# Moving GpSimd's word load behind a gather, and building the second pass's edge one-hots from TensorE's squares

## The chip, the cores and the metric

The kernel runs on one core of a Trainium2 chip. The metric is device time in microseconds. The kernel before takes 11216.39 us (median of 3 runs, 11213.91 to 11227.2); the execution that was profiled took 11191.52 us, and its span in the trace is 11189.8 us.

## The reference

Four graph layers over 6250 nodes of 128 features and 200,000 edges, sorted by destination. Each layer is `x = x + layer(relu(layernorm(x)))`. Their edge work, cut to what matters:

```python
# layer 0: typed attention, 4 heads         # layer 1: GAT, 4 heads
a   = (kw[e] * q[dst]).sum(-1) * pri        a = leaky_relu(a_src[src] + a_dst[dst], 0.2)
att = exp(a - max_dst(a)) / sum_dst         att = exp(a - max_dst(a)) / sum_dst
agg = segment_sum(msg * att, dst)           out = segment_sum(xh[src] * att, dst)
# layer 2: graph convolution                # layer 3: clipped attention, 8 heads
agg = segment_sum(h[src] * deg, dst)        s = exp(clip(K[src].Q[dst] / 4, -5, 5)); sum V[src] * s
```

Between them stand dense products over the 49 blocks of 128 nodes.

## The kernel before, in words

**Four edge passes.** Each layer has one pass over all edges: `softmax_pass` for layers 0 and 1 (called with `dot` true and false), `conv_pass` for layer 2, `clipped_pass` for layer 3. Edges come in 392 groups of 512, each group in four tiles of 128. A group whose edges end in more than one block of 128 destination nodes is visited once for each block, so there are 440 visits. Every engine has a program of its own, unrolled over 12 or 16 visits in a loop, and they are coupled by semaphores alone.

**GpSimd's program (`fetch`, L449).** For each of the 392 groups it issues four indirect gathers (L464), one for each tile of 128 edges, from a table in DRAM (`kv_typed`, `gat_rows`, `conv_rows`, `kv_rows`) into one of 14 slots of a ring in SBUF (`edges_rows`). Behind each gather stands a `pause` (L467), an addition on a tile of 128x56. That makes 1568 gathers and as many pauses in a pass. A slot may be filled again when the visits that read it are over. How many visits that is depends on the data, and stands in a table in SBUF (`seat_rows`). At the first group of each half ring (7 groups) GpSimd's sequencer loads 7 of these words into registers (`TENSOR_LOAD`, L377), and then waits, ahead of each group, for the semaphore `used` to reach the group's word. The loop runs over 14 groups, so half of the loads stand at the head of a turn of the loop.

**A visit of the softmax passes.** TensorE multiplies five feature rows per edge (`feat_r`) with a constant (`col_feat`): the result in `ps_near` is the squared distance of each edge's destination from each of the 128 nodes (`squares`, L587). ScalarE turns it into a one-hot, `relu(1 - x)`, with nodes in the partitions (`pick_tb`, L705, and for `dot` also `pick_t`). The other orientation, with edges in the partitions (`pick_b`), is made by VectorE: it compares a row 0..127 with each edge's local number (`make_pick`, L754; the tile lies in the space of `x` in the first pass and of `q` in the second). ScalarE widens `pick_b` to f32 (`widen_pick`, L665) for the sums that TensorE makes eight visits later (`sum_rows`, L615); VectorE adds them to the running sums (L812) after fading these (L806). In the second pass VectorE also makes one-hots that count the sources (`count`, L897), and weighs the gathered rows (`weigh`, L797). VectorE works through a visit in the order that `body` at L899 writes out.

## Time and profile before

| | busy us | share of the span |
|---|---|---|
| GpSimd (POOL) | 8748.9 | 78% |
| TensorE (PE) | 6661.3 | 60% |
| VectorE (DVE) | 5435.4 | 49% |
| ScalarE (ACT) | 2291.9 | 20% |
| span / time of the profiled execution | 11189.8 / 11191.52 | |

Busy counts the engine itself. Loads of registers, branches, semaphores and the issuing of DMAs are the sequencer's and not counted, so they show only as idle time of the engine ahead of its next instruction. For GpSimd, a gather (`DMA_INDIRECT`) is counted as busy. The passes are found by the table that the gathers read: the first gather of a pass starts, and the last one ends, at 537.3 and 3009.2 us (layer 0), 3187.1 and 5834.2 (layer 1), 6024.5 and 8469.1 (layer 2), 8631.8 and 11075.1 (layer 3).

### The profile page before, as it was taken

To read this page: it belongs to the slowest core of one execution; us is meant where nothing else is said; L and a number is where in the kernel's file an instruction comes from. 1 tells how busy PE (TensorE), PEld (TensorE's weight loads), DVE (VectorE), ACT (ScalarE), POOL (GpSimd) and SP (SyncE) were. 2 spreads that over 40 slices of the span, in tenths; PEclk is the share of its full clock that TensorE was granted. 3 is DMA by queue.
4 is the path that set the end of the run, shared out by engine and by line. 5 is a ranking of instruction groups with operands and counts; after the bars stand their busy time and mean duration, and the time that the engine had idled before them with its cause. 6 is when DMAs were issued, how large, how long until landed. Compare 5 with 4: busy or idle time off the path is not lost. (4 is left out here: it accounts for less than half of the span.)

```text
span 11189.8 us, 165217 instructions
## 1 busy us (share of the span) xinstructions
PE 6661.3 (60%) x36530; PEld 5305.4 (47%) x36531; DVE 5435.4 (49%) x14242; ACT 2291.9 (20%) x6368; POOL 8748.9 (78%) x12683
## 2 busy tenths in 40 slices
PE   5867777777755555555554333333336767776767
PEld 3656556556534444444443333333333555555554
DVE  4266666666666565566554111111113555555555
ACT  1333333333342222222223000000002111111111
POOL 0188888888758888888876888888883888888885
PEclk9966666767765555555556555555555666666667
DMA  3332222222211111111121111111111332222222
GB/s 114 141 87 84 85 85 85 85 86 85 78 43 42 42 42 41 42 42 43 42 49 34 43 43 42 43 43 43 43 43 52 87 86 85 85 85 85 85 85 65
DMA packets 379796, 731.69 MB, mean 65 GB/s; under 512 B 169786, under 2 KB 219249, under 8 KB 373270
## 3 DMA queue, kind: packets, MB, share of 16 engines
q0 software_dynamic: 251264, 621.88, 21.3%
q1 hardware_dynamic: 100906, 98.01, 2.7%
q10 hardware_dynamic: 27500, 10.39, 0.4%
q8 instruction: 46, 0.75, 0.0%
q14 instruction: 80, 0.66, 0.0%
HBM read 652.95 MB, written 76.88 MB: 65 GB/s over the span
## 5 line engine op out<-in xcount | busy, mean ns | idle before, releaser
L467 POOL TENSOR_TENSOR edges_pause<-edges_pause 128x56 f32<-128x56 f32 x6272 | 2094.7, 334 | 120.0
L464 POOL DMA_INDIRECT edges_rows<-gat_rows,edges_idx_r x1568 | 1743.7, 1112 | 326.2 <-issue 301.8
L464 POOL DMA_INDIRECT edges_rows<-conv_rows,edges_idx_r x1568 | 1628.7, 1039 | 331.7 <-issue 320.6
L464 POOL DMA_INDIRECT edges_rows<-kv_typed,edges_idx_r x1568 | 1596.3, 1018 | 332.6 <-issue 313.5
L1005 PE MATMUL edges_ps_sum<-edges_rows,edges_pick 128*128 x3520 | 889.1, 435 | 1580.5 <-POOLq L470 1551.9
L464 POOL DMA_INDIRECT edges_rows<-kv_rows,edges_idx_r x1568 | 1520.5, 970 | 332.1 <-issue 322.7
L615 PE MATMUL edges_ps_sum<-edges_wv,edges_pick 128*128 128x132 f32 x7040 | 1676.2, 410 | 30.1 <-issue 17.6
L615 PEld LDWEIGHTS edges_ps_sum<-edges_wv,edges_pick 128*128 128x128 f32 x7040 | 1433.4, 298 | 368.4 <-issue 340.2
L1005 PEld LDWEIGHTS edges_ps_sum<-edges_rows,edges_pick 128*128 128x128 f32 x3520 | 773.6, 325 | 1695.8 <-issue 1695.7
L1103 PE MATMUL edges_ps_q<-q,edges_pick_t 128*128 x3520 | 751.8, 381 | 726.2 <-DVE edges_prod L1167 644.1
L1025 DVE TENSOR_TENSOR sums<-sums,edges_ps_sum 128x129 f32 x440 | 127.7, 290 | 2038.8 <-PE edges_ps_sum L1005 1684.3
L1103 PEld LDWEIGHTS edges_ps_q<-q,edges_pick_t 128*128 128x128 f32 x3520 | 650.6, 276 | 828.6 <-issue 828.1
L1093 PE MATMUL edges_ps_sum<-edges_wv,edges_pick 128*128 128x136 f32 x3520 | 810.1, 399 | 7.9 <-DVE sums L1189 7.8
L597 PE MATMUL edges_ps_q<-q,edges_pick_t 128*128 x3520 | 760.9, 379 | 58.9 <-issue 40.0
L1093 PEld LDWEIGHTS edges_ps_sum<-edges_wv,edges_pick 128*128 128x128 f32 x3520 | 693.4, 284 | 164.7 <-issue 161.6
L597 PEld LDWEIGHTS edges_ps_q<-q,edges_pick_t 128*128 128x128 f32 x3520 | 658.7, 277 | 96.1 <-issue 89.9
L797 DVE TENSOR_TENSOR edges_wv<-edges_rows,edges_wv 128x512 f32<-128x512 f32 x880 | 618.3, 703 | 1.5 <-ACT edges_wv L657 1.4
L1167 DVE TENSOR_TENSOR edges_prod<-edges_rows,edges_ps_q 128x512 f32<-128x512 f32 x440 | 301.6, 685 | 620.6 <-issue 339.7
L1157 DVE TENSOR_TENSOR edges_pick<-edges_ps_iota,edges_local 128x512 f32<-128x512 f32 x440 | 304.5, 692 | 546.5 <-issue 516.5
L754 DVE TENSOR_TENSOR x<-iota_bf,edges_local 128x512 bf16<-128x512 bf16 x440 | 314.4, 714 | 481.3 <-issue 398.0
L1134 ACT ACTIVATE edges_wv<-edges_gap 128x32 f32<-128x32 f32 x440 | 113.1, 257 | 2123.4 <-DVE edges_gap L1196 1756.4
L657 ACT ACTIVATE edges_wv<-edges_gap 128x16 f32<-128x16 f32 x880 | 200.8, 228 | 1543.8 <-issue 1149.9
(343 smaller groups left out, 10567.2 us busy)
## 6 DMA issues: line engine op xcount, KB each, us to landing
kv_typed<-l0pre_out SPq DMA_DIRECT2D x49, 1024.0 KB
edges_rows<-kv_typed,edges_idx_r POOLq DMA_INDIRECT x1568
edges_rows<-gat_rows,edges_idx_r POOLq DMA_INDIRECT x1568
edges_rows<-conv_rows,edges_idx_r POOLq DMA_INDIRECT x1568
edges_rows<-kv_rows,edges_idx_r POOLq DMA_INDIRECT x1568
edges_feat_r<-visit_features ACTq DMA_DIRECT2D x660, 10.0 KB
kv_rows<-l3pre_kv SPq DMA_DIRECT2D x7, 896.0 KB
edges_flag_r<-visit_flags ACTq DMA_DIRECT2D x220, 16.0 KB
```

The costliest lines, as they stand in the source:

```text
L464: pool.indirect_dma_start(rows[:, k, g * width:(g + 1) * width], None, table, bass.IndirectOffsetOnAxis(ap=idx_r[:, k, g:g + 1], axis=0)). ...
L467: nc.gpsimd.tensor_tensor(pause, pause, pause, ALU.add).then_inc(paused, 1)
L597: mm = nc.tensor.matmul(ps_q[s % 2][:, g * D:(g + 1) * D], pick_t[:, s % 2, g * P:(g + 1) * P], q[:, bass.ds(b * D, D)], start=True, stop= ...
L615: mm = nc.tensor.matmul(ps_sum[s % 2][:, 0:aw], pick[:, s % 2, g * P:(g + 1) * P], wv[:, s % 3, g, :], start=g == 0, stop=g == G - 1)
L657: nc.scalar.activation(wv4[:, s % 3, :, :, hd], gap[:, s // SPAN, j * GH:(j + 1) * GH].rearrange("p (g h) -> p g h", g=G), ACT.Exp).then_i ...
L754: nc.vector.tensor_tensor(pick_b[:, s, :].rearrange("p (g n) -> p g n", g=G), c["iota_bf"].unsqueeze(1).broadcast_to([P, G, P]), bcast(loc ...
L797: nc.vector.tensor_tensor(wv4[:, s % 3, :, :, 0:hd], vals, bcast(wv4[:, s % 3, :, :, hd], [P, G, heads, hd]), ALU.mult).then_inc(wv_done, 1)
L1005: mm = nc.tensor.matmul(ps_sum[k % banks][:, 0:aw], pick[:, k % deep, g * P:(g + 1) * P], now[:, g, :], start=g == 0, stop=g == G - 1)
L1093: mm = nc.tensor.matmul(ps_sum[s % 2][:, 0:aw], pick[:, s % 6, g * P:(g + 1) * P], wv[:, s % 3, g, :], start=g == 0, stop=g == G - 1)
L1103: mm = nc.tensor.matmul(ps_q[s % 2][:, g * D:(g + 1) * D], pick_t[:, s % 2, g * P:(g + 1) * P], q[:, bass.ds(b * D, D)], start=True, stop= ...
L1157: nc.vector.tensor_tensor(pick[:, s % 6, :].rearrange("p (g n) -> p g n", g=G), ps_iota[:, 0:P].unsqueeze(1).broadcast_to([P, G, P]), bcas ...
L1167: nc.vector.tensor_tensor(prod[:].rearrange("p (g d) -> p g d", g=G), of_slot(rows, slot, width)[:, :, 0:D], ps_q[s % 2][:].rearrange("p ( ...
```

## The change

Two things. First, in `fetch` the load of the words moves behind the first gather of the half ring, ahead of that gather's pause. It then holds the words of the next seven groups, and not of the half ring's own. The first group of a half ring waits for nothing any more: its word is waited for one group earlier (`k % HALF == HALF - 1`), in place of that group's own, smaller word. This holds for all four passes.

Second, in the second pass (`dot` false) VectorE no longer makes `pick_b`. TensorE makes a second set of squares, transposed, from the same feature rows: four products of 128 columns into a new bank `ps_pick`, and ScalarE turns it into `pick_b` with a second activation. There is now one bank `ps_near` in that pass instead of two, squares are made two visits ahead instead of three, and `local` is not loaded.

```diff
@@ fetch
         if k % HALF == 0:
             pool.wait_ge(idx_in[k // HALF], it * 16 + 16)
-            if known(j, SLOTS):
-                visits[:] = words(pool, res, 3, j - SLOTS, HALF)
-        if known(j, SLOTS):
-            pool.wait_ge(used, at_least_one(pool, visits[k % HALF], NV))
+        elif k % HALF == HALF - 1 and known(j + 1, SLOTS):
+            pool.wait_ge(used, at_least_one(pool, visits[HALF - 1], NV))
+        elif known(j, SLOTS):
+            pool.wait_ge(used, at_least_one(pool, visits[k % HALF - 1], NV))
         pool.sem_inc(slot_free, 1)
         for g in range(G):
             pool.indirect_dma_start(...)
+            if g == 0 and k % HALF == 0 and known(j + HALF, SLOTS):
+                early = max(SLOTS - 1 - j, 0) if isinstance(j, int) else 0
+                visits[:] = [None] * early + list(words(pool, res, 3, j + 1 - SLOTS + early, HALF - early))
             pool.wait_ge(paused, j * G + (g + 1))
             nc.gpsimd.tensor_tensor(pause, pause, pause, ALU.add).then_inc(paused, 1)
@@ softmax_pass, tensor: squares
-                    if known(u, 2):
-                        pe.wait_ge(pick_tb_done, u - 1)
-                    nc.tensor.matmul(ps_near[s % 2][:], c["col_feat"], feat_r[:, s // 2 % 3, s % 2], start=True,
-                                     stop=True).then_inc(squares_done, 1)
+                    near = feat_r[:, s // 2 % 3, s % 2]
+                    if known(u, near_banks):
+                        pe.wait_ge(pick_tb_done, u + 1 - near_banks)
+                        if not dot:
+                            pe.wait_ge(pick_b_done, u)
+                    mm = nc.tensor.matmul(ps_near[s % near_banks][:], c["col_feat"], near, start=True, stop=True)
+                    if not dot:
+                        for g in range(G):
+                            mm = nc.tensor.matmul(ps_pick[:, g * P:(g + 1) * P], near[:, g * P:(g + 1) * P], c["col_feat"], start=True, stop=True)
+                    mm.then_inc(squares_done, 1)
-                    to_square, to_spread, last, ninth = (wide_at(i, k, it, d) for d in (3, 1, -1, -9))
+                    to_square, to_spread, last, ninth = (wide_at(i, k, it, d) for d in (3 if dot else 2, 1, -1, -9))
@@ softmax_pass, scalar: one_hots
                     if s % SPAN == 0 and known(u, WIDE):
                         act.wait_ge(ref_done, t * 3 + s // SPAN - 2)
+                        if not dot:
+                            act.wait_ge(top_part, t * 3 + s // SPAN - 2)
-                    nc.scalar.activation(pick_tb[:, s, :], ps_near[s % 2][:], ACT.Relu, bias=1.0, scale=-1.0).then_inc(pick_tb_done, 1)
+                    nc.scalar.activation(pick_tb[:, s, :], ps_near[s % near_banks][:], ACT.Relu, bias=1.0, scale=-1.0).then_inc(pick_tb_done, 1)
+                    if not dot:
+                        nc.scalar.activation(pick_b[:, s, :], ps_pick[:], ACT.Relu, bias=1.0, scale=-1.0).then_inc(pick_b_done, 1)
@@ softmax_pass, vector
-                    if now:
+                    if dot and now:
                         make_pick(now)
-                    if dot and now:
                         multiply_q(now, slot, due)
-                dve.wait_ge(local_in, 16)
+                if dot:
+                    dve.wait_ge(local_in, 16)
```

GpSimd's program at the head of a turn of the second pass's loop, before. `ISA` rows are arithmetic on registers, `L377` belongs to the words, `L386` checks a word and waits with it:

```order
L467 TENSOR_TENSOR edges_pause<-edges_pause 128x56
L367 UNCONDITIONAL_BRANCH
L367 BRANCH_PREFETCH_HINT
L367 ISA
L377 ISA
L377 TENSOR_LOAD seat_rows
L386 ISA x2
L464 DMA edges_rows<-gat_rows,edges_idx_r 128x132
L466 ISA
L467 TENSOR_TENSOR edges_pause<-edges_pause 128x56
```

The same place now:

```order
L470 TENSOR_TENSOR edges_pause<-edges_pause 128x56
L367 UNCONDITIONAL_BRANCH
L367 BRANCH_PREFETCH_HINT
L367 ISA
L464 DMA edges_rows<-gat_rows,edges_idx_r 128x132
L377 ISA
L377 TENSOR_LOAD seat_rows
L469 ISA
L470 TENSOR_TENSOR edges_pause<-edges_pause 128x56
L464 DMA edges_rows<-gat_rows,edges_idx_r 128x132
```

The load stood between a pause and a gather; it stands between a gather and its pause.

VectorE's program for one visit of the second pass, before (L754 is `make_pick`, L806 the fading, L897 the source counts, L797 the weighing):

```order
L377 TENSOR_LOAD seat_rows
L754 TENSOR_TENSOR q<-iota_bf,edges1_local 128x512
L806 ISA
L806 TENSOR_TENSOR sums<-sums,edges1_fade 128x132
L897 TENSOR_TENSOR edges1_lo_hot<-iota_bf,edges1_src_lo 128x512
L897 TENSOR_TENSOR edges1_hi_hot<-iota_bf,edges1_src_hi 128x196
L797 ISA
L797 TENSOR_TENSOR edges1_wv<-edges1_rows,edges1_wv 128x16x32
L821 TENSOR_TENSOR edges1_ends<-edges1_ps_turn,last_rows 128x64
L812 TENSOR_TENSOR sums<-sums,edges1_ps_sum1 128x132
```

The same visit now (all lines behind the changed ones are numbered 16 higher):

```order
L377 TENSOR_LOAD seat_rows
L822 ISA
L822 TENSOR_TENSOR sums<-sums,edges1_fade 128x132
L913 TENSOR_TENSOR edges1_lo_hot<-iota_bf,edges1_src_lo 128x512
L913 TENSOR_TENSOR edges1_hi_hot<-iota_bf,edges1_src_hi 128x196
L813 ISA
L813 TENSOR_TENSOR edges1_wv<-edges1_rows,edges1_wv 128x16x32
L837 TENSOR_TENSOR edges1_ends<-edges1_ps_turn,last_rows 128x64
L828 TENSOR_TENSOR sums<-sums,edges1_ps_sum1 128x132
```

Only `make_pick` is gone there. TensorE's program for a visit of the second pass, now, in which the row L599 is new:

```order
L616 MATMUL edges1_ps_q<-a_dst,q 128x12 x4
L596 MATMUL edges1_ps_near0<-edges1_feat_r,col_feat 128x512
L599 MATMUL edges1_ps_pick<-col_feat,edges1_feat_r 128x128 x4
L627 MATMUL edges1_ps_sum1<-edges1_wv,edges1_pick 128x132 x4
L635 MATMUL edges1_ps_hist<-edges1_hi_hot,edges1_lo_hot 128x49 x4
```

The four new products stand between the squares and the sums.

## Rows read from the trace of the kernel before

**Rows 1.** The passes: length; PE, PEld, DVE, ACT, POOL busy; clock, DMA share, GB/s.
```profile
537.30:3009.20 2471.90, 1782.65 (x11088) 1445.76 (x11086) 1602.56 (x4231) 835.89 (x2175) 2113.51 (x3135) 0.68 0.30 85
3187.10:5834.20 2647.10, 1488.05 (x11111) 1190.08 (x11111) 1588.83 (x4905) 720.18 (x2173) 2297.22 (x3135) 0.50 0.19 42
6024.50:8469.10 2444.60, 886.97 (x3512) 771.78 (x3512) 402.53 (x878) 0.00 (x0) 2087.65 (x3135) 0.52 0.19 43
8631.80:11075.10 2443.30, 1713.17 (x7447) 1374.21 (x7447) 1274.99 (x2628) 323.41 (x878) 2084.24 (x3135) 0.65 0.30 85
```

**Rows 2.** GpSimd by line, each pass: busy us, mean ns, idle ahead and its releasers.
```profile
L464 POOL DMA_INDIRECT edges_rows<-kv_typed,edges_idx_r x1568 | 1596.3, 1018 | 332.6 <-issue 313.5 <-DVE edges_wv L797 15.0 <-DMA edges_idx_r<-typed_sources 4.1
L467 POOL TENSOR_TENSOR edges_pause<-edges_pause 128x56 f32<-128x56 f32 x1567 | 517.3, 330 | 29.9
...
L464 POOL DMA_INDIRECT edges_rows<-gat_rows,edges_idx_r x1568 | 1743.7, 1112 | 326.2 <-issue 301.8 <-DVE edges_wv L797 17.1 <-DMA edges_idx_r<-sources 6.8
L467 POOL TENSOR_TENSOR edges_pause<-edges_pause 128x56 f32<-128x56 f32 x1567 | 553.6, 353 | 30.4
...
L464 POOL DMA_INDIRECT edges_rows<-conv_rows,edges_idx_r x1568 | 1628.7, 1039 | 331.7 <-issue 320.6 <-PE edges_ps_sum L1005 6.8 <-DMA edges_idx_r<-sources 4.4
L467 POOL TENSOR_TENSOR edges_pause<-edges_pause 128x56 f32<-128x56 f32 x1567 | 459.0, 293 | 29.6
...
L464 POOL DMA_INDIRECT edges_rows<-kv_rows,edges_idx_r x1568 | 1520.5, 970 | 332.1 <-issue 322.7 <-DVE edges_wv L1174 6.3 <-DMA edges_idx_r<-sources 3.1
L467 POOL TENSOR_TENSOR edges_pause<-edges_pause 128x56 f32<-128x56 f32 x1567 | 563.8, 360 | 30.0
```

**Rows 3.** Waits of GpSimd's gathers, whole span: us, times, longest us.
```profile
POOL edges_rows L464 <- DVE edges_wv L797: 32.1, 20, 1.8
```

**Rows 4.** Line 377, word loads (ns min/median/max, start): all; the one before 6588.
```profile
L377 POOLq TENSOR_LOAD <-seat_rows x216: 1591/1601/1808, 618.8 to 11031.7; - x108
...
L377 POOLq TENSOR_LOAD <-seat_rows x1: 1594/1594/1594, 6587.0 to 6587.0; - x1
```

**Rows 5.** Timeline (start, us, idle ahead) of GpSimd, load inside a turn.
```profile
6585.64 0.96 POOL L464 DMA_INDIRECT edges_rows<-conv_rows,edges_idx_r  x1 [0.16 <-issue]
...
6587.06 0.96 POOL L464 DMA_INDIRECT edges_rows<-conv_rows,edges_idx_r  x1 [0.16 <-issue]
6588.04 0.29 POOL L467 TENSOR_TENSOR edges_pause<-edges_pause 128x56 f32<-128x56 f32 x1
6589.65 0.96 POOL L464 DMA_INDIRECT edges_rows<-conv_rows,edges_idx_r  x1 [1.33 <-issue]
```

**Rows 6.** The same around a load at the head of a turn.
```profile
6981.36 0.96 POOL L464 DMA_INDIRECT edges_rows<-conv_rows,edges_idx_r  x1 [0.16 <-issue]
...
6984.42 1.42 POOL L464 DMA_INDIRECT edges_rows<-conv_rows,edges_idx_r  x1 [1.79 <-PE edges_ps_sum L1005]
```

**Rows 7.** Timeline of the second pass, GpSimd and VectorE in a long gather.
```profile
4034.69 3.32 POOL L464 DMA_INDIRECT edges_rows<-gat_rows,edges_idx_r  x1 [1.74 <-DVE edges_wv L797]
4034.82 0.67 DVE L754 TENSOR_TENSOR q<-iota_bf,edges_local 128x512 bf16<-128x512 bf16 x1
4035.42 0.28 DVE L806 TENSOR_TENSOR sums<-sums,edges_fade 128x132 f32 x1
...
4037.66 0.23 DVE L830 TENSOR_TENSOR edges_split<-edges_ends,edges_split 128x64 bf16<-128x64 f32 x1
```

**Rows 8.** Groups by line in the second pass.
```profile
L754 DVE TENSOR_TENSOR q<-iota_bf,edges_local 128x512 bf16<-128x512 bf16 x440 | 309.2, 703 | 191.8 <-issue 148.4 <-ACT edges_pick L665 43.4
...
L587 PE MATMUL edges_ps_near<-edges_feat_r,col_feat 5*128 5x512 bf16 x440 | 264.8, 602 | 0.0
L705 ACT ACTIVATE q<-edges_ps_near 128x512 bf16<-128x512 f32 x440 | 258.4, 588 | 92.0 <-issue 71.3 <-PE edges_ps_near L587 20.5
```

**Rows 9.** Timeline of TensorE in the second pass, its sums of consecutive pairs.
```profile
4032.29 2.13 PE L615 MATMUL edges_ps_sum<-edges_wv,edges_pick 128*128 128x132 f32 x8
...
4035.80 2.13 PE L615 MATMUL edges_ps_sum<-edges_wv,edges_pick 128*128 128x132 f32 x8
```

11 lines of the change are left out of this document (7 added, 4 removed).

## The prediction

> **What bounds the kernel now.** I read the busy shares first: GpSimd has 78% of the span. Then the passes one by one. In each of the four GpSimd is busy for 2084 to 2297 us of 2443 to 2647, 85 to 87%, and every other engine for at most 72% [rows 1]. Next, GpSimd's own groups: a pass is 1568 gathers and their pauses, the means are 970 to 1112 ns and 293 to 360 ns, and the idle time ahead of the gathers is "issue", not a wait for somebody's work [rows 2]. Check: 1743.7 + 553.6 + 326.2 + 30.4 = 2653.9, the second pass with the 6.8 us ahead of its first gather. The waits that are put down to VectorE's `edges_wv` are 20 in the span and none is over 1.8 us [rows 3]; these are 1.8 us because a word load stands there, as the next views show. So GpSimd runs back to back, the passes last as long as its stream, and a microsecond taken out of it shortens the kernel. The chain that ended last tells nothing here, as it covers only the last dense stage.
>
> GpSimd's beat is read in the timeline: from gather to gather 6587.06 - 6585.64 = 1.42 us, with 0.16 us idle ahead of a gather [rows 5]. Ahead of the first gather of a half ring it is idle for 1.33 us inside a turn of the loop [rows 5] and 1.79 at its head [rows 6]. The cause is the word load: 216 of them, all about 1.60 us [rows 4]. The sequencer issues it when the gather before starts (6587.0 against 6587.06 [rows 4, 5]), so 1.26 us of it lie beside that gather and its pause; it ends at 6588.6, and the next gather starts 1.04 us behind that.
>
> **Term A, the load, in all four passes.** Before, 54 loads a pass: 27 at (1.33 - 0.16) and 27 at (1.79 - 0.16) are 31.6 + 44.0 = 75.6 us. The other way round, from [rows 2] for the third pass: 331.7 - 4.4 (its first wait) - 1568 x 0.16 = 76.4. Both agree; in the second pass it is 326.2 - 6.8 - 250.9 = 68.5, as its long gathers cover some of it.
> After: the load stands behind a gather and ahead of its pause, in program order. The gather is issued, the load starts with it as before (0.04 us ahead) and ends at 1.56 us on the gather's clock; one register instruction and the pause's dispatch, 0.1 us estimated, put the pause at 1.66 to 1.70 in place of 0.98 (6588.04 - 6587.06). It delays the next gather by 0.70 us. The first gather of the half ring itself now follows at 0.16: the loop's branch and the wait for the indices, 0.46 us (1.79 - 1.33), lie beside a gather and a pause of 1.26. There is one more load (group 7, one word): 55 x 0.70 = 38.5 us a pass. Saved: 75.6 - 38.5 = 37 us in three passes and 68.5 - 38.5 = 30 in the second, together 141 us. So the move does not take away the load; it drops the tail of 1.04 us behind it for 0.1 us and the branch in its shadow, but gives up the pause as cover.
> Bounds: nothing is paid for the tail or the pause waits for nothing of the load: 4 x 75 = 295 us. If the load's tail of 1.04 us goes along with it, the delay is 1.56 + 1.04 - 1.42 + 0.28 + 0.16 = 1.62 us, 55 x 1.62 = 89 a pass, and A is a loss of 4 x 14 = 54 us. I take 141: no gather's address and no check of a word stands between load and pause now, as the order shows.
> The wait for a later word, one group early, costs nothing: GpSimd does not wait for a word today [rows 3]. What hides it is a ring of 14 slots; if that cover were gone, each half ring would wait for up to one group, 4 x 1.42 = 5.7 us.
>
> **Term B, VectorE off GpSimd's back, in the second pass.** VectorE's `make_pick` is 440 x 703 ns = 309 us [rows 8]. VectorE is busy for 60% of this pass [rows 1], so that alone buys nothing. But GpSimd's own instructions are stretched: the gathers' mean is 1112 ns against 1039 in the third pass, whose table has rows of nearly the same width (132 and 129 words), and the pauses' 353 against 293 [rows 2]: 1568 x 0.073 + 1567 x 0.060 = 114 + 94 = 208 us. A gather of 3.32 us shows how: it starts at 4034.69, VectorE starts `make_pick` at 4034.82 and then works without a break until 4037.89, and the gather ends at 4038.01, 0.12 us behind [rows 7]; the usual is 0.96 [rows 5]. In that chain `make_pick` is 0.67 of 3.07 us, 22%. If the stretching shrinks with VectorE's time, B = 0.22 x 208 = 46 us. If the second pass becomes like the first, it is more: the first against the fourth (two tables of rows of 256 words) is 1568 x 0.048 - 1567 x 0.030 = 28 us, so nearly all of 208 would go, the upper end. The lower end: the third pass, too, has a `make_pick` a visit and the stretching is measured against it, so that `make_pick` alone may be worth nothing. I take 60, above the proportional 46, because `make_pick` is what the break in VectorE's work is missing: it opens the chain, and without it VectorE waits there.
> The Trainium skill ("SBUF — State Buffer", Who interferes with whom) says that a VectorE instruction with two inputs in SBUF holds GpSimd up only where that reads SBUF, and infers that the writing of descriptors is not held by such a one. The trace disagrees with the second half, with its gather of 3.32 us [rows 7]. By the rule only the pauses would gain, 0.22 x 94 = 21 us in place of 60.
>
> **Term C, the new work.** TensorE: four products of 128 columns, as many columns as the one of 602 ns [rows 8], 0.6 us a visit and 264 us in all; ScalarE: one more activation of 588 ns [rows 8], 259 us. With them TensorE is busy for 1750 of 2600 us and ScalarE for 980. When rows have come, TensorE goes through its visits at 35.80 - 32.29 = 3.5 us each [rows 9]; this becomes 4.1, while GpSimd delivers a visit each 2647 / 440 = 6.0 us. So the work is hidden by 1.9 us a visit, and costs 0.6 x 10 visits, at most 6 us, in the tail behind the last gather. I take 3. What the cover is worth: each 0.1 us by which a visit passes 6.0 costs 44 us.
>
> **Sum.** 141 + 60 - 3 = 198 us off the profiled execution's 11191.5: 10993. The median is 25 us above that execution, and I carry that along: 11216 - 198 = 11018 us. A difference under 0.2%, 22 us, counts as no change.
>
> **Rivals.**
> 1. *The load carries its tail along.* A is -54, B 60: 11216 - 3 = 11213, no change. For it: today every gather behind a load comes 1.04 us late. Against: that tail holds the check of a word and the gather's address, and neither stands behind the load now. Chance 0.07.
> 2. *The port is freed for good.* VectorE's chains break up, B is 150: 11216 - 141 - 150 + 3 = 10928. For it: the first pass has no such stretching. Against: the source counts and the weighing stay, 2.4 of the chain's 3.07 us. Chance 0.14.
> 3. *`make_pick`'s place is taken by what follows it.* B is 0 to 20: 11216 - 141 - 10 + 3 = 11068. For it: GpSimd meets another VectorE instruction at once. Against: the chain is shorter in any case. Chance 0.17. The Trainium skill's rule above ("SBUF — State Buffer", Who interferes with whom) would leave the gathers as they are and so points to this case.
> 4. *Slower: the single bank makes the second pass TensorE's.* TensorE may write `ps_near` only when ScalarE has read both banks of the visit before. If squares (1.2 us), two activations (1.2) and the sums with their rest (2.9) came one behind the other with waits between, a visit would take over 6.0 us and GpSimd would wait for slots. At 6.8 us the pass lasts 440 x 6.8 = 2992, 345 more than 2647: 11216 + 345 - 111 (A of the other passes) = 11450. It decides from 6.02 us. Against: ScalarE reads the squares in the visit in which TensorE makes them and the next come one visit later, so the sums lie between. Chance 0.03.
>
> **How the numbers follow.** The forecast, 10975 to 11055, has 0.56; rival 1 0.07, 2 0.14, 3 0.17, 4 0.03; the remaining 0.03 is a load wholly hidden, 11216 - 295 - 60 + 3 = 10864. The range 10925 to 11115 takes in rivals 2 and 3 at their times and leaves out 1, 4, the hidden load and a part of 2. Faster: 0.56 + 0.14 + 0.17 + 0.03 and a quarter of rival 1, 0.92; same 0.05; slower 0.03.
>
> **What would show it.** In the second pass, `ps_pick` products and a second activation; GpSimd's idle time ahead of its gathers at 250 to 262 us a pass, and that ahead of the pauses at 30 + 38 = 68 (before 30); in the timeline a pause 0.7 us behind its gather's end each half ring. Gathers and pauses of the other three passes unchanged in length; in the second, gathers under 1.09 us and pauses under 0.34. The passes at 2435, 2557, 2408 and 2406 us. It is wrong if the idle time only moves from gathers to pauses (rival 1), if the gathers of the second pass stay above 1.10 us (rival 3), or if GpSimd waits for `used` there (rival 4).

## The result and the profile after

The changed kernel takes 10847.47 us (median of 4 runs, 10836.52 to 10850.32), the kernel before 11218.1 beside it. The ratio is 0.9667, 95% interval 0.965 to 0.9683: faster by 371 us, where 198 were forecast. The time lies below the forecast range. The profiled execution took 10849.15 us, its span is 10847.4. The trace of the kernel before is of an execution of 11191.52 us that is not among the four runs behind those 11218.1, so differences of a few us between the two traces can be those of two chips.

The table of passes of the changed kernel answers to [rows 1], with the same columns:

```profile
537.20:2944.70 2407.50, 1748.33 (x11088) 1424.08 (x11086) 1605.28 (x4231) 838.30 (x2175) 2110.58 (x3135) 0.70 0.30 87
3121.00:5558.00 2437.00, 1644.74 (x12746) 1325.34 (x12746) 1372.00 (x4419) 931.36 (x2591) 2102.94 (x3135) 0.50 0.20 46
5766.60:8166.80 2400.20, 889.66 (x3512) 774.37 (x3512) 402.92 (x878) 0.00 (x0) 2111.68 (x3136) 0.52 0.20 44
8330.90:10730.90 2400.00, 1720.68 (x7446) 1378.65 (x7447) 1274.36 (x2628) 323.31 (x878) 2096.64 (x3135) 0.65 0.30 87
```

The passes are shorter by 64, 210, 44 and 43 us; what lies between and behind them is longer by 20. So 152 us come from the three passes that only the load's move touches, and 210 from the second. Forecast were 37, 90, 37 and 37: of the 161 us between 201 and 362, 120 lie in the second pass and 27 in the first.

GpSimd by line in each pass answers to [rows 2] (busy us, mean ns, idle ahead and its releasers):

```profile
L464 POOL DMA_INDIRECT edges_rows<-kv_typed,edges_idx_r x1568 | 1604.6, 1023 | 264.5 <-issue 260.2 <-DMA edges_idx_r<-typed_sources 4.2
L470 POOL TENSOR_TENSOR edges_pause<-edges_pause 128x56 f32<-128x56 f32 x1567 | 506.0, 323 | 36.6 <-issue 6.7
...
L464 POOL DMA_INDIRECT edges_rows<-gat_rows,edges_idx_r x1568 | 1573.5, 1004 | 304.8 <-issue 258.9 <-DVE edges_wv L813 40.0 <-DMA edges_idx_r<-sources 5.6
L470 POOL TENSOR_TENSOR edges_pause<-edges_pause 128x56 f32<-128x56 f32 x1567 | 529.5, 338 | 34.9 <-issue 4.9
...
L464 POOL DMA_INDIRECT edges_rows<-conv_rows,edges_idx_r x1568 | 1649.9, 1052 | 262.9 <-issue 258.3 <-DMA edges_idx_r<-sources 4.4
L470 POOL TENSOR_TENSOR edges_pause<-edges_pause 128x56 f32<-128x56 f32 x1568 | 462.0, 295 | 30.1 <-issue 0.3
...
L464 POOL DMA_INDIRECT edges_rows<-kv_rows,edges_idx_r x1568 | 1525.2, 973 | 269.1 <-issue 265.1 <-DMA edges_idx_r<-sources 3.9
L470 POOL TENSOR_TENSOR edges_pause<-edges_pause 128x56 f32<-128x56 f32 x1567 | 571.5, 365 | 38.2 <-issue 8.6
```

Three things are to be seen. The idle time ahead of the gathers fell by 63 to 69 us in the first, third and fourth pass, to 259 to 265 without the few us for the indices: with 1568 gaps of 0.16 us (251) almost nothing of the load is left there. The pauses' idle time rose by 0.5 to 8, not by the 38 forecast. And in the second pass the gathers' mean fell from 1112 to 1004 ns and the pauses' from 353 to 338, 170 + 24 = 194 us. In the kernel before, 53 gathers of that pass were over 1 us longer than its shortest one; now it is 1. But 40.0 us are waits of a new kind for VectorE's `edges_wv`. The 17.1 before lay at word loads and none was over 1.8 us [rows 3]; now there are 15 of up to 4.5 us, in which GpSimd waits for free slots of the ring.

In the third pass the gathers and pauses grew by 21 + 3 us, so that of 68 us less idle time 44 arrive. (Some 15 of the 24 come with the load's move on one chip too: 2088 us with the load in its old place and 2103 in the new one, in b_only and load_twice below.)

The new work of the second pass, against [rows 8] (L599 is TensorE's transposed squares, L719 and L721 ScalarE's two activations):

```profile
L599 PE MATMUL edges_ps_pick<-col_feat,edges_feat_r 5*128 5x128 bf16 x1748 | 275.6, 308 | 3.6 <-issue 3.4
...
L719 ACT ACTIVATE q<-edges_ps_near 128x512 bf16<-128x512 f32 x437 | 261.0, 597 | 1157.2 <-PE edges_ps_pick L599 551.5 <-remote 498.1 <-issue 107.0
L721 ACT ACTIVATE q<-edges_ps_pick 128x512 bf16<-128x512 f32 x437 | 258.4, 591 | 0.0
```

Now the load inside a turn of the loop, in the timeline of GpSimd (start, us, idle ahead; answers to [rows 5]), and ahead of it the load's own row:

```profile
L377 POOLq TENSOR_LOAD <-seat_rows x1: 1604/1604/1604, 1437.9 to 1437.9; - x1
```

```profile
1437.38 0.96 POOL L464 DMA_INDIRECT edges_rows<-kv_typed,edges_idx_r  x1 [0.16 <-issue]
1438.37 0.29 POOL L470 TENSOR_TENSOR edges_pause<-edges_pause 128x56 f32<-128x56 f32 x1
1438.81 1.00 POOL L464 DMA_INDIRECT edges_rows<-kv_typed,edges_idx_r  x1 [0.16 <-issue]
1439.84 0.47 POOL L470 TENSOR_TENSOR edges_pause<-edges_pause 128x56 f32<-128x56 f32 x1
1440.46 0.96 POOL L464 DMA_INDIRECT edges_rows<-kv_typed,edges_idx_r  x1 [0.15 <-issue]
...
1824.59 0.29 POOL L470 TENSOR_TENSOR edges_pause<-edges_pause 128x56 f32<-128x56 f32 x1
1825.03 0.96 POOL L464 DMA_INDIRECT edges_rows<-kv_typed,edges_idx_r  x1 [0.16 <-issue]
1826.35 0.28 POOL L470 TENSOR_TENSOR edges_pause<-edges_pause 128x56 f32<-128x56 f32 x1 [0.36 <-issue]
1827.03 1.04 POOL L464 DMA_INDIRECT edges_rows<-kv_typed,edges_idx_r  x1 [0.40 <-issue]
```

The load stands in program order behind the gather of 1438.81, and yet it starts at 1437.9, 0.9 us before it: the sequencer hands a gather over while the one before is still at work, and runs on to the load. It ends at 1439.50, before the pause is due at 1439.84, so inside a turn it costs nothing. At the head of a turn (the rows behind the "...", against [rows 6]) the branch comes first, the load starts at 1824.6, 0.46 us before its gather, and the pause and the next gather are late by 0.36 - 0.02 and 0.40 - 0.16 us: 0.58 us, at most 27 times a pass, 16 us. The fall from 75.6 to 16 us would be 60 a pass; the idle times ahead of gathers and pauses together fell by 61, 68 and 55 us in the first, third and fourth pass.

### The profile page after: what moved, and what is told of

Its sections match the earlier page's. It is cut to its first block and busy times, and to the rows that moved or that the text cites. A ratio compares the mean times of both kernels' runs of the same rounds, so it can differ in the third digit from the quotient of the medians.

```text
span 10847.4 us, 168021 instructions
## 1 busy us (share of the span) xinstructions
PE 6808.6 (63%) x38290; PEld 5435.5 (50%) x38291; DVE 5233.5 (48%) x13802; ACT 2512.3 (23%) x6808; POOL 8588.5 (79%) x12683
## 5 line engine op out<-in xcount | busy, mean ns | idle before, releaser
L470 POOL TENSOR_TENSOR edges_pause<-edges_pause 128x56 f32<-128x56 f32 x6272 | 2069.9, 330 | 139.9 <-issue 20.5
L464 POOL DMA_INDIRECT edges_rows<-gat_rows,edges_idx_r x1568 | 1573.5, 1004 | 304.8 <-issue 258.9
L1119 PE MATMUL edges_ps_q<-q,edges_pick_t 128*128 x3520 | 754.9, 382 | 675.7 <-DVE edges_prod L1183 664.4
L609 PE MATMUL edges_ps_q<-q,edges_pick_t 128*128 x3520 | 732.4, 373 | 25.8 <-DVE edges_prod L780 11.7
L913 DVE TENSOR_TENSOR edges_lo_hot<-iota_bf,edges_src_lo 128x512 bf16<-128x512 bf16 x440 | 313.1, 712 | 562.9 <-remote 455.6
```

What stands on the lines that cost most here:

```text
L464: pool.indirect_dma_start(rows[:, k, g * width:(g + 1) * width], None, table, bass.IndirectOffsetOnAxis(ap=idx_r[:, k, g:g + 1], axis=0)). ...
L470: nc.gpsimd.tensor_tensor(pause, pause, pause, ALU.add).then_inc(paused, 1)
L609: mm = nc.tensor.matmul(ps_q[s % 2][:, g * D:(g + 1) * D], pick_t[:, s % 2, g * P:(g + 1) * P], q[:, bass.ds(b * D, D)], start=True, stop= ...
L913: ins = nc.vector.tensor_tensor(hot[:, s % 2], c["iota_bf"][:, 0:n].unsqueeze(1).broadcast_to([P, G, n]), bcast(digits[:, bass.ds(u * G, G ...
L1119: mm = nc.tensor.matmul(ps_q[s % 2][:, g * D:(g + 1) * D], pick_t[:, s % 2, g * P:(g + 1) * P], q[:, bass.ds(b * D, D)], start=True, stop= ...
```

## The experiments

The kernels ran on five chips in turn, which I call B to F; the kernels of one group ran on one chip. A is that of the result, whose chip is not on record: it may be one of the five. "Before" took 11181 to 11205 us on all of them, but the changed kernel did not take one time, as the table says. "Waits" are those of GpSimd's gathers for `edges_wv` in the second pass. The 13 of b_only and the 44 of b_only_again are no more than at word loads, like the 17 before: none is over 1.9 us, and the idle time ahead of the gathers in that pass, 327 and 328 us, is as in the other passes with the load in its old place (325 to 330 in b_only). The ratio is to the kernel before on the same chip.

| kernel | chip | us | ratio, 95% interval | second pass | waits |
|---|---|---|---|---|---|
| changed | A | 10847.47 | 0.9667, 0.965 to 0.9683 | 2437 | 40 |
| a_only | B | 10998.29 | 0.9816, 0.9799 to 0.9832 | 2625 | 0 |
| b_only | B | 10973.3 | 0.9793, 0.9777 to 0.981 | 2452 | 13 |
| load_twice (as changed) | B | 10827.67 | 0.9667, 0.965 to 0.9683 | 2449 | 64 |
| load_behind_second_gather | B | 10852.25 | 0.9682, 0.9666 to 0.9699 | 2494 | 133 |
| load_both | C | 11367.34 | 1.0169, 1.0152 to 1.0186 | 2687 | see text |
| no_pick | C | 11098.22 | 0.9933, 0.9916 to 0.9949 | 2611 | 254 |
| pick_two_inputs | C | 11060.75 | 0.9901, 0.9883 to 0.992 | 2548 | 0 |
| pick_one_input | C | 11111.27 | 0.9946, 0.9929 to 0.9962 | 2628 | 232 |
| changed_again | D | 11151.76 | 0.9952, 0.9935 to 0.9969 | 2676 | 328 |
| no_pick_again | D | 11087.25 | 0.9889, 0.9872 to 0.9905 | 2608 | 242 |
| a_only_more_pe | D | 11018.3 | 0.9844, 0.9827 to 0.986 | 2554 | 0 |
| mixed | D | 11134.04 | 0.9939, 0.9922 to 0.9956 | 2613 | 234 |
| changed_third | E | 10717.91 | 0.9575, 0.9559 to 0.959 | 2362 | 0 |
| b_only_again | E | 10929.22 | 0.9767, 0.975 to 0.9783 | 2421 | 44 |
| half_sums | E | 10720.62 | 0.9579, 0.9563 to 0.9595 | 2362 | 0 |
| fewer_hots | E | 10718.18 | 0.9579, 0.9563 to 0.9595 | 2366 | 0 |
| changed_fourth | F | 11169.93 | 0.9962, 0.995 to 0.9974 | 2699 | 352 |
| half_sums_again | F | 11118.01 | 0.9923, 0.9906 to 0.9939 | 2623 | 270 |

### The two parts by themselves

**a_only**: only `fetch` is changed; TensorE, ScalarE and VectorE work as before.

```diff
-                    if dot and now:
+                    if now:
                         make_pick(now)
```

> Only the first part of the change: the word load behind the first gather, in all four passes; the second pass keeps VectorE's make_pick. My theory (run-ahead): GpSimd's sequencer has issued the half ring's first gather while the engine still works on the gather before it, so the load starts 0.5 to 0.9 us before that first gather and not with it. It costs nothing inside a turn of the loop and 0.6 us at its head. Then this kernel saves 64, 44 and 43 us in the first, third and fourth pass, as the changed kernel does, and about 50 in the second: 11218 - 201 = 11017 us, with 43 + 18 long gathers and pauses in the second pass as before. By the prediction's term A (the load starts with the gather) it would save 141: 11077. Rival: the long gathers of the second pass come from where the load stands; then they vanish here too and it saves some 370.

Measured: 207 us faster than before. Passes 1, 3 and 4 take 2402, 2396 and 2392 us, like those of the changed kernel; the second takes 2625, with its gathers at a mean of 1146 ns (before 1112 [rows 2]) and 103 of them over 1 us longer than the shortest, where I expected 43 as before. So the first part is worth 207 in place of 141, and it does nothing for the stretched gathers: there are more of them, and the second pass is only 22 us shorter than before.

**b_only**: only the second part; `fetch` as before.

```diff
+            if known(j, SLOTS):
+                visits[:] = words(pool, res, 3, j - SLOTS, HALF)
...
-            if g == 0 and k % HALF == 0 and known(j + HALF, SLOTS):
```

> Only the second part: edge one-hots of the second pass from TensorE's squares, the word load where it was. My theory: what was gained in the second pass beyond the load is VectorE's make_pick off GpSimd's back, so the gathers of that pass are at 1.00 to 1.02 us as in the changed kernel, and the pass loses 150 to 165 us: 11218 - 155 = 11063. The tail behind the pass's last gather is longer by 10 to 20 us. By the prediction's term B it would be 60: 11160. Rival: the long gathers vanish because the beat of GpSimd changed against VectorE's; then nothing is gained here and the tail makes it 10 us slower.

Measured: 232 us faster. That is more than the 155 I expected. The gathers' mean in the second pass is 997 ns, one is over 1 us longer than the shortest. 207 + 232 = 439 is more than the 377 that both give on this chip (load_twice): 62 us are given back. Where they are lost shows when load_twice is set beside b_only, which differ by the load's place alone: it shortens the first, third and fourth pass by 55, 51 and 57 us and the second by only 4, in which 64 us are waits for slots, and the stretch behind the second pass grows by 18.

### The load's place and price

**load_behind_second_gather**:

```diff
-            if g == 0 and k % HALF == 0 and known(j + HALF, SLOTS):
+            if g == 1 and k % HALF == 0 and known(j + HALF, SLOTS):
```

> The changed kernel with the word load behind the second gather of a half ring in place of the first. Run-ahead theory: at the head of a turn the load starts only 0.46 us before its gather, since the loop's branch stands ahead, and GpSimd loses 0.6 us there, about 27 times a pass; one gather later it has the full 0.9 us of run-ahead and costs nothing: 4 x 27 x 0.6 = 65 us less than the changed kernel, 10780 to 10800. Rival (registers are filled in the background, and only their first use waits): the place doesn't matter, as the words are used a group later in both, and it stays at 10847.

Measured: the first, third and fourth pass take 2399, 2387 and 2377 us, which is 0, 6 and 17 less than with the load behind the first gather on this chip (2399, 2393, 2394), and not 16 each. The idle time ahead of gathers and pauses did fall in all three, by 13, 7 and 16 us, so behind the second gather the load costs less at the head of a turn too; in the first pass the pauses took 13 us longer. But the second pass took 2494 in place of 2449, with 133 us of waits for slots in place of 64, and the sum is 25 us worse, where 47 to 67 less than 10847 were expected.

**load_twice**: the load written twice, with nothing between.

> The changed kernel with every word load done twice in a row. Run-ahead theory: the sequencer stands still for the length of a load, 1.60 us, and the first has used up the run-ahead; the second is paid in full, 220 x 1.6 = 350 us: about 11200. Rival (the load is in the background until first use): two loads are over 3.2 us after they start, and the first use is a group, 5.7 us, later; nothing is added, 10847.

The trace has 220 loads, as many as the changed kernel: one of each pair is not in the program that ran. So this is a run of the changed kernel, and it says nothing of the price of a second load.

**load_both**: the second load's words are used for waits of their own, so it stays.

```diff
             pool.wait_ge(used, at_least_one(pool, visits[k % HALF - 1], NV))
+            pool.wait_ge(used, at_least_one(pool, again[k % HALF - 1], NV))
...
                 visits[:] = [None] * early + list(words(pool, res, 3, j + 1 - SLOTS + early, HALF - early))
+                again[:] = [None] * early + list(words(pool, res, 3, j + 1 - SLOTS + early, HALF - early))
```

> The changed kernel with each word load done twice into two sets of registers, both of which are waited for (in load_twice the compiler had dropped the second load, as its registers were the only ones used: 220 loads in the trace as before). Run-ahead theory: the sequencer stands still for 1.60 us in a load; the first one uses up the run-ahead and the second is paid in full wherever GpSimd sets the pace: about 55 x 1.6 = 88 us in the first, third and fourth pass; less in the second, where GpSimd waits for others by now: 10845 + 264 + 40 = 11150. Some 15 us come on top for the doubled checks. Rival (loads run in the background until first use): under 20 us more.

Measured: 11367 us, 217 more than expected. GpSimd by line in its second pass (busy, mean, idle ahead), and its loads:

```profile
L466 POOL DMA_INDIRECT edges_rows<-gat_rows,edges_idx_r x1568 | 1562.4, 996 | 506.0 <-issue 500.3 <-DMA edges_idx_r<-sources 5.5
L473 POOL TENSOR_TENSOR edges_pause<-edges_pause 128x56 f32<-128x56 f32 x1567 | 508.6, 325 | 115.1 <-issue 85.7
```

```profile
L377 POOLq TENSOR_LOAD <-seat_rows x440: 271/1593/1614, 577.7 to 11196.9; - x147
```

The pauses' idle time is 115 us in place of 35: the second load is paid almost whole, 80 us / 55 = 1.45 of 1.60 us. The third and fourth pass take 2478 and 2485 us in place of 2400 in the result, 78 and 85 more, against the 88 expected. So loads don't run in the background; the first one is free only because of the sequencer's lead over the engine. (Here the waits for slots are two instructions and the rows put them down to "issue": of the 500 us, some 240 are more than in the changed kernel. They, and a first pass of 2502 us, are what the expectation lacked.)

### Is it VectorE's second input in SBUF that stretches the gathers?

**pick_two_inputs**: the changed kernel, but `make_pick` is VectorE's again, without the transposed squares. **pick_one_input**: the same, with the row 0..127 read from PSUM, so that only one input is in SBUF. **no_pick**: nobody makes `pick_b`, it stays zero; there are two banks `ps_near` and squares three visits ahead, as before. The edit of pick_one_input beside pick_two_inputs, and that of no_pick:

```diff
-                                            c["iota_bf"].unsqueeze(1).broadcast_to([P, G, P]),
+                                            (c["iota_bf"] if dot else ps_pick[:, 0:P]).unsqueeze(1).broadcast_to([P, G, P]),
```

```diff
-                        for g in range(G):
-                            mm = nc.tensor.matmul(ps_pick[:, g * P:(g + 1) * P], near[:, g * P:(g + 1) * P], c["col_feat"], start=True, stop=True)
...
+                    nc.vector.memset(pick_b, 0.0).then_inc(zeroed, 1)
```

> The changed kernel, but in the second pass VectorE makes pick_b again from a row and numbers in SBUF, with one bank ps_near and squares two visits ahead (the control for pick_one_input). Port theory: the long gathers are back, about 100 of them over 1.9 us, pass 2625: 10998, the same as a_only. Rival (the fewer banks or the shorter lead took the long gathers away): 10800.

> As pick_two_inputs, but VectorE reads the row 0..127 from a bank of PSUM of its own, so make_pick has one input in SBUF instead of two; it takes as long. Port theory (a VectorE instruction with two SBUF inputs holds GpSimd up, and make_pick closes the gap between two stretches of such instructions): no long gathers, as in the changed kernel, and TensorE is spared the new products: second pass 2400, total 10790. Rival (VectorE's unbroken work as such stretches the gathers, whatever its inputs): as pick_two_inputs, 10998.

> The changed kernel without the new work of the second pass: nobody makes pick_b (it is set to zero once and the sums of layer 1 are left out in effect), two banks ps_near, squares three visits ahead. Theory (TensorE paces the second pass): the changed kernel's second pass is 2437 us, more than the 2400 of the third and fourth, because TensorE with the new products falls behind and GpSimd waits for slots (40 us on edges_wv). Without them the pass takes 2390 to 2405 and the tail behind it is 18 us shorter: 10845 - 38 - 18 = 10790. Rival (the wait for the next group's word one group early makes these waits): they stay, and the time is 10845.

GpSimd's gathers and VectorE's `make_pick` in the second pass, two inputs:

```profile
L464 POOL DMA_INDIRECT edges_rows<-gat_rows,edges_idx_r x1568 | 1733.6, 1106 | 263.5 <-issue 256.6 <-DMA edges_idx_r<-sources 6.7
...
L760 DVE TENSOR_TENSOR q<-iota_bf,edges_local 128x512 bf16<-128x512 bf16 x440 | 307.9, 700 | 193.6 <-issue 149.0 <-ACT edges_pick L671 44.5
```

One input:

```profile
L464 POOL DMA_INDIRECT edges_rows<-gat_rows,edges_idx_r x1568 | 1578.3, 1007 | 496.7 <-issue 256.9 <-DVE edges_wv L807 232.4 <-DMA edges_idx_r<-sources 6.7
...
L764 DVE TENSOR_TENSOR q<-edges_ps_pick,edges_local 128x512 bf16<-128x512 f32 x436 | 299.5, 687 | 185.5 <-issue 168.4 <-ACT edges_pick L671 16.8
```

The instruction is as long and as frequent, but with one input from PSUM the gathers' mean falls from 1106 to 1007 ns and the long ones from 42 to 1; without it at all (no_pick) the mean is 983. So 155 of 192 us hang on the second input from SBUF, and not on VectorE's busy time.

The kernel with one input also waits for slots, and with two it does not, so the pace could be the reason in place of the input. Taking the gathers one by one rules that out. Of those that have `make_pick` at work 0.1 us behind their start, the 125 with two inputs take 1706 ns in the mean and hold all 42 long ones; the 182 with one input take 972 ns, hardly more than with an idle VectorE (959 in both). Of those that have the first one-hot of the source count at work there, 317 take 1375 and 153 take 1312 ns: that instruction kept its two inputs, and it stretches gathers in both kernels. It still holds up pauses too: with one input for `make_pick` 20 pauses are over 1 us longer than the shortest, with two 4.

The total did not follow: what GpSimd won in its gathers it lost as waits for slots (232 us), and on this chip the kernel with the stretched gathers was the fastest of the three.

### Why the time depends on the chip

**changed_again**, **no_pick_again**, **a_only_more_pe** (a_only with eight small products more per visit of the second pass) and **mixed** (new one-hots; in the second pass the load in its old place, in the others behind the second gather) ran on chip D. The edit of a_only_more_pe, beside a_only's, and that of mixed:

```diff
+                        for _ in range(8):
+                            nc.tensor.matmul(ps_near[s % 2][:, 0:4], c["col_feat"], feat_r[:, s // 2 % 3, s % 2, 0:4], start=True, stop=True)
```

```diff
+            if not ahead and known(j, SLOTS):
+                visits[:] = words(pool, res, 3, j - SLOTS, HALF)
...
-            if g == 0 and k % HALF == 0 and known(j + HALF, SLOTS):
+            if ahead and g == 1 and k % HALF == 0 and known(j + HALF, SLOTS):
```

> The changed kernel once more, beside the three that follow, since in no_pick, pick_two_inputs and pick_one_input the first pass, whose code is the changed kernel's, took 2456 to 2485 us and not 2400 to 2407. If those runs tell of the kernels, it is at 10830 to 10850 again, its first pass at 2400 to 2410. If they tell of the place where they ran, it shows the same slow first pass here.

> no_pick once more, on the same chip as changed_again. Theory (TensorE falls behind in the second pass once GpSimd's gathers are no longer stretched, whether or not it has the new products): its second pass is at 2600 with over 200 us of waits for slots again, 11080 in all. Rival (the runs of that batch were disturbed): 10790, as first expected.

> a_only with eight small products of 4 columns per visit of the second pass, written into ps_near ahead of the squares and overwritten by them; TensorE's work grows by some 0.3 us a visit, its instructions from 25 to 33. In the changed kernel TensorE's signals (squares, sums, counts) come at the median 1.0 to 2.1 us behind the end of their record, in the kernel before 0.01. Theory (late signals come with the number of TensorE's instructions): lateness over 1 us here and a second pass over 2650. Rival (they come with a GpSimd that is not stretched, so that the slots fill and VectorE's and TensorE's visits run without a break): no lateness, the long gathers stay, 11000 as a_only.

> A version to beat the changed kernel: in passes 1, 3 and 4 the word load behind the second gather, where it has the whole run-ahead; in the second pass the load where it was before the change, so that GpSimd does not outrun the visits there, with the new one-hots. From load_behind_second_gather (first, third, fourth pass 2399, 2387, 2377) and b_only (second pass and its tail 2452 + 189, against 2437 + 209 in the changed kernel): 2399 + 2387 + 2377 against 2407 + 2400 + 2400 is 44 us less, the second pass 5 less: 10800. Rival (the second pass is as long as GpSimd's stream in any case, so the old place costs 30 us): 10830.

The same program that took 10847 and 10828 us took 11152 here. Against the trace of the result the second pass is 239 us longer, the first 47, and what lies outside the passes 36; the first and the fourth pass have waits for slots too (25 and 48 us), the third has none. GpSimd's gathers in its second pass:

```profile
L464 POOL DMA_INDIRECT edges_rows<-gat_rows,edges_idx_r x1568 | 1551.8, 990 | 585.7 <-DVE edges_wv L813 328.3 <-issue 251.1 <-DMA edges_idx_r<-sources 5.7
```

The gathers are as short as they should be; 328 us are waits for slots. The timeline of that pass shows who is late (TensorE's squares of a visit, then ScalarE, which reads them):

```profile
4409.49 0.58 PE L596 MATMUL edges_ps_near<-edges_feat_r,col_feat 5*128 5x512 bf16 x1 [0.22 <-issue]
...
4409.87 0.63 PE L599 MATMUL edges_ps_pick<-col_feat,edges_feat_r 5*128 5x128 bf16 x4
...
4418.48 0.60 ACT L719 ACTIVATE q<-edges_ps_near 128x512 bf16<-128x512 f32 x1 [5.12 <-remote]
```

TensorE's products end at 4410.50 by the records, and ScalarE, idle for 5.12 us, starts on them at 4418.48, 8 us later, 0.02 us behind the semaphore's increment in the trace. The next increments of TensorE, in the order of its program, are late as well (that of the sums by 7.4 us, at 4419.99 for an end at 4412.55), so it is the whole engine that is behind its records there, and their busy time is not the time that its work took. The trace holds 1998 of the 2166 increments that TensorE's records call for in that pass. Matched to the records in their order, half of them come over 1 us late and a fifth over 4 us. The Trainium skill ("Perfetto Trace Analysis", Tensor Engine Instruction) says that the end of a product is estimated from its size and that the semaphore goes up when PSUM has acknowledged the write; the trace agrees, as it is the increment that the readers follow. a_only_more_pe, with 14631 products in that pass in place of 11111, has no such waits and takes 2554 us there, and no_pick_again, with 10999 products, waits for 242 us, so it is not the number of products alone. mixed did not help either: 2613 us, 234 of waits.

On chip E I ran the changed kernel beside one with less work for TensorE (**half_sums**: two of the four sum products of a visit left out), one with less for VectorE (**fewer_hots**: the larger one-hot of the source count left out) and **b_only_again**.

```diff
-                    for g in range(G):
+                    for g in range(G) if dot else (0, G - 1):
```

```diff
-                    for hot, digits, n in ((lo_hot, src_lo, P), (hi_hot, src_hi, NT)):
+                    for hot, digits, n in ((hi_hot, src_hi, NT),):
```

> The changed kernel as it is, for its time beside the three others on one chip. So far it took 10847 and 10828 us on two chips and 11152 on a third, with GpSimd waiting for ring slots in the second pass for 40, 87 and 328 us. Theory 1 (TensorE, at the lower of its two clock levels there, is the bound of the second pass whenever GpSimd runs unhindered): waits for slots of 40 to 330 us again, with TensorE's semaphores posted over 1 us behind the recorded ends in about half of the cases. Theory 2 (VectorE's chain is the bound): the same waits, so this run alone tells nothing apart.

> The changed kernel, which in the second pass leaves out two of the four sum products of each visit (TensorE only; part of the sums of that layer is missing). Theory 1 (TensorE is the bound): GpSimd's waits for slots go to near 0, late posts under 10 in 100 over 4 us become none, and the second pass comes to 2390 to 2410 us on any chip. Theory 2 (VectorE or ScalarE is the bound, TensorE's posts are late for another reason): the second pass within 20 us of the unchanged one's.

> The changed kernel, which in the second pass leaves out the larger of the two one-hots for the source count (VectorE only, about 0.71 us of 3.1 a visit, 310 us in all; the count is then wrong). Theory 1 (TensorE is the bound): the waits for slots stay within 50 us of the unchanged kernel's. Theory 2 (VectorE is the bound): they go to near 0 and the second pass to about 2400 us.

> The second part of the change alone (one-hots from TensorE's squares), the word load in its old place, which holds GpSimd to one visit's rows each 5.6 us or slower. Theory 1 with a limit that lies close to this pace: on a chip where the changed kernel waits for 300 us this one waits too, 50 to 250 us, and takes as long in the second pass as the changed kernel; on a chip where that waits for under 90 us this one waits for none and the pass takes 2450 us. Theory 2 expects the same of the time; it is told apart by the two runs before.

Here the changed kernel took 10718 us, 474 less than before. Its passes (columns as in [rows 1]) and the same place in the timeline:

```profile
535.90:2922.40 2386.50, 1739.60 (x11088) 1423.22 (x11087) 1591.88 (x4231) 839.57 (x2176) 2086.25 (x3135) 0.70 0.31 88
3099.70:5461.50 2361.80, 1632.65 (x12871) 1341.51 (x12871) 1359.00 (x4466) 945.24 (x2613) 2062.94 (x3135) 0.50 0.22 47
5650.10:8045.00 2394.90, 890.41 (x3512) 774.96 (x3512) 402.68 (x878) 0.00 (x0) 2104.25 (x3135) 0.52 0.20 44
```

```profile
4401.65 0.63 PE L599 MATMUL edges_ps_pick<-col_feat,edges_feat_r 5*128 5x128 bf16 x4
...
4402.31 0.60 ACT L719 ACTIVATE q<-edges_ps_near 128x512 bf16<-128x512 f32 x1 [0.69 <-PE edges_ps_pick L599]
```

ScalarE starts 0.03 us behind the recorded end. All increments of TensorE in this run are 14 ns behind the ends (9 in 10 at most 15), GpSimd never waits for a slot, and the second pass is the shortest of the four. With nobody late, less work for TensorE or VectorE changes nothing (10720.6 and 10718.2 us), so theories 1 and 2 are not told apart here. b_only_again is 263 us faster than before, and the load's move on top of it is worth 211: 47, 59, 48 and 55 us in the four passes, so that here the second pass has its full share. The load's move alone did not run on this chip.

One more thing sets chip E apart. The trace of the changed kernel there holds 40036 updates of semaphores in the second pass; on the other chips it holds 15800 to 17000, all four traces of chip E are near 40000, and the kernel before has 22424. So where TensorE is late, the profile also loses over half of these records; in the third pass, where it is late in no trace, the changed kernel's traces hold 21600 to 23200 of some 29600. Whether taking the profile is what slows the engine, or both have one cause, no run tells, as every time on record is of an execution with a span and clocks from the profiler.

The last pair, on chip F, tried it again on a chip with late increments.

> The changed kernel once more, beside one with less of TensorE's work. On a chip whose TensorE posts its semaphores at once (as where it took 10718 us) I expect 10700 to 10740 us and no wait for ring slots; on one where it posts them 1 to 8 us late, 10820 to 11160 us with 40 to 330 us of such waits in the second pass.

> The changed kernel without two of the four sum products of each visit of the second pass (part of the sums of that layer is missing). On a chip with late posts: if the amount of TensorE's work makes them late (theory 1), the second pass comes to 2360 to 2410 us and its waits for slots to under 20 us; if another cause holds TensorE up (theory 2), both stay within 20% of the unchanged kernel's. On a chip without late posts the two kernels take the same time, which would leave it open.

GpSimd's gathers and TensorE's sums in the second pass, the changed kernel:

```profile
L464 POOL DMA_INDIRECT edges_rows<-gat_rows,edges_idx_r x1568 | 1552.2, 990 | 609.7 <-DVE edges_wv L813 351.7 <-issue 252.0 <-DMA edges_idx_r<-sources 5.8
L627 PE MATMUL edges_ps_sum<-edges_wv,edges_pick 128*128 128x132 f32 x3408 | 912.2, 448 | 10.2 <-issue 9.8
```

With half of the sums:

```profile
L464 POOL DMA_INDIRECT edges_rows<-gat_rows,edges_idx_r x1568 | 1549.2, 988 | 530.4 <-DVE edges_wv L813 269.6 <-issue 254.7 <-DMA edges_idx_r<-sources 5.6
```

Taking 364 us of TensorE's recorded busy time out of the pass (1658.7 to 1295.1) shortens it by 76 and the waits by 82 us; 21 in 100 increments are over 4 us late with all sums and 26 with half. So the amount of TensorE's work is a part of it, and not the cause: on chip E the same products are done in a pass of 2362 us without one late increment. The fall of 82 of 352 us is just over the 20% that I had set as theory 2's limit, and far from theory 1's, so neither is confirmed.

## Why the prediction was wrong

**What held.** GpSimd's stream sets the time, in every pass and for both parts, but for the waits for slots told of below. Rival 1 is out: the idle time ahead of the gathers went and did not come back at the pauses. Term C held: TensorE's 276 us and ScalarE's 258 us of new work [rows 8] are hidden; on chip E they cost nothing that can be seen, and the stretch between the second and the third pass (188.6 us) is no longer than before. On chip A it grew by 18 us, where I had 3: at the last gather of the pass TensorE has recorded 12746 products in place of chip E's 12871, some four visits less, which fits a ring that is full there.

Two of the prediction's bounds have slips that change neither its sum nor its range: 4 x 75 is 300 (from the terms above it is 295), and the loss of rival 1 by its own terms is 61 us, not 54.

**Term A failed in the step "the load starts with it as before (0.04 us ahead)".** I took the load to run beside the gather behind which it is written. But the sequencer hands that gather over one instruction early, so the load starts 0.9 us ahead of it inside a turn and 0.46 at its head. It costs 0 and 0.58 us, not 0.70 and 0.70: at most 16 us a pass in place of 38.5. The rows for it stood in the prediction: by [rows 4, 5] the load, written behind the pause of 6588.04, started at 6587.0, 1.04 us ahead of that pause, and I gave it no such lead over the instruction that it now stands behind. Alone the part is worth 207 us (chip B), on top of the other part 146 (B) and 211 (E); 141 were predicted.

**Term B failed in "I take 60".** The 208 us of stretching were sized rightly, and so was the upper end: in the result 194 of them are gone, and alone the part is worth 232 and 263 us. I let the gain go by `make_pick`'s share in the chain's time (0.22). Measured, hardly a gather is over 1 us too long without it, though the other two-input instructions (the source count, the weighing) remained: those still stretch the gathers that start beside them (1160 ns beside the count's first one-hot in the result, 962 beside an idle VectorE), but by less than 0.5 us in nearly all. In the trace before, 47 of the 53 long gathers have `make_pick` at work 0.1 us behind their start and the count at 0.9 us. So a long one seems to need two such instructions in a row, which no run tests by itself. Rival 2 (the port freed for good, B = 150, chance 0.14) was the right mechanism, its size too small; rival 3, to which I gave 0.17, was wrong. The rule of the Trainium skill ("SBUF — State Buffer", Who interferes with whom) names the right cause, two inputs in SBUF, as pick_one_input shows with 1007 against 1106 ns. I had read its inference, that the writing of descriptors is not held up by them, as one for the whole gather, and the traces contradict that reading (a gather of 3.32 us [rows 7], 42 long gathers with two inputs and 1 with one). They don't tell whether it is the writing of descriptors that waits: a gather also reads its indices, `edges_idx_r`, from SBUF, and for a reader of SBUF the rule expects a wait.

**Rival 4 (GpSimd waits for slots, chance 0.03) is in part what happens,** on the chips with late increments. "It decides from 6.02 us a visit": on chip D the pass takes 2676 / 440 = 6.08 us a visit, and GpSimd waits for 328 us. The mechanism given, the single bank, is not it: no_pick keeps two banks and waits for 254 us. On chip A these waits took back up to 40 us, on B 64.

**The sum.** On chip E 263 + 211 = 474 us, which holds by the way in which the 211 were taken. On chip A 371; by the two traces, idle time without slot waits 224 us less, gathers and pauses of the second pass 194 less, those of the other passes 34 more, waits for `edges_wv` 23 more (40.0 against 17.1 us [rows 2]), and the stretches outside the passes 20 more, together the spans' 342.

**What stays open.** What makes TensorE late on every chip but E: in the second pass of the changed kernel 20 and 21 in 100 increments are over 4 us late on D and F, 10 and 11 on B and A. It goes together with a profile that loses records (see above), and the runs don't separate the two. The granted clock does not tell them apart (0.50 in the second pass everywhere). The late increments are there in the trace of the kernel before too (first pass: median 2.1 us), where GpSimd is too slow for it to matter. The chip alone does not set them either: in the fourth pass, whose code is the same, they have a median of 4.8 us in changed_again and of 0.015 us in a_only_more_pe, both on chip D. On chips C and D the kernels whose gathers are stretched have none over 4 us in the second pass (pick_two_inputs 19 and a_only_more_pe 23 in 100 over 1 us) and no waits for slots, though the number of products is as in the kernel before or higher. Why TensorE is more punctual where GpSimd is slower stays open.

No version beat the changed kernel where it is at its best. On chip D a_only_more_pe, the fetch change with the old one-hots, took 11018 us against 11152 for both changes: there the second part costs more than it brings.

## What to carry to other kernels

Where an engine's sequencer and the engine itself run apart, find out which instruction the sequencer is at before pricing something that only the sequencer does: behind an instruction that is handed over early, 1.6 us of register loads cost nothing, and the second such load costs 1.45. When gathers on GpSimd are stretched, look for VectorE instructions with both inputs in SBUF that start with them, and move one input to PSUM or the work to another engine; price it by the whole stretching, not by the instruction's share. And when the engine that was the bound becomes faster, run the result on several chips: one and the same program differed by 452 us between them here.

## What the runs showed of the hardware that I had not expected

- GpSimd's sequencer is up to one gather ahead of the engine: a load written behind a gather starts 0.9 us before that gather does, and 0.46 us behind a branch. It blocks the sequencer for 1.60 us all the same (load_both: the pauses' idle time 35 to 115 us a pass).
- One program takes 10718, 10828, 10847, 11152 and 11170 us in five places (four chips, and that of the result), each within 0.6% by itself, while the kernel before takes 11181 to 11218 in all of them.
- A gather that has a VectorE instruction with both inputs in SBUF at work 0.1 us behind its start takes 1706 ns in the mean (`make_pick`), against 972 ns when one of the inputs is in PSUM and 959 when VectorE is idle.
- TensorE's semaphores go up 14 ns behind the recorded end on one chip; on others, in the second pass of the changed kernel, the median is 1.1 to 1.4 us and one in ten is over 4 to 6 us late. The readers wait for the semaphore. A row "<-remote" with a TensorE product long done is the sign of it, and those traces hold less than half of the semaphore updates that the punctual chip's does.
